# Routing of a fused transformer front: comparison numbers in PSUM, ranks by groups of five tiles, the experts' table on GpSimd

## What is computed

```python
h = tok(x, ...)                                  # patches, class token, positions
h = concatenate([h, txt], axis=1)                # 64 x 69 x 256
h = h + attn(layernorm(h), wq, wk, wv)
h = h + ffn(layernorm(h), router, w13, w2)

# ffn: the two best of eight experts, weighted by a softmax over the two logits
router_logits = x_flat @ moe_router              # 4416 x 8
topk_logits, topk_idx = top_k(router_logits, 2)
topk_weights = softmax(topk_logits)
sort_idx = argsort(topk_idx.reshape(-1))         # 8832 pairs, grouped by expert
w13_out = ragged_dot(x_sort, moe_w13, group_sizes)
hidden = silu(gate) * up
out = ragged_dot(hidden, moe_w2, group_sizes)    # added back to the token's row
```

## Time and profile before

| What | us |
|---|---|
| median of 3 runs | 825.34 |
| lowest and highest run | 822.24, 830.76 |
| the profiled execution, its own time | 829.55 |
| its span, first to last instruction | 827.4 |
| TensorE busy | 724.2 (88%) |
| VectorE busy | 552.7 (67%) |
| ScalarE busy | 418.2 (51%) |
| GpSimd busy | 435.6 (53%) |

### The profile page before, as it was taken

How to read it: one execution, slowest core, us unless ns; L and a number is a source line. 1 busy time by engine, 2 the same in 40 slices (tenths; PEclk the granted TensorE clock), 3 DMA queues, 4 the chain that set the end, 5 groups by cost and what they waited for, 6 DMA issues and landing times. The chain is left out here.

```text
span 827.4 us, 27945 instructions
## 1 busy us (share of the span) xinstructions
PE 724.2 (88%) x9928; PEld 511.9 (62%) x9928; DVE 552.7 (67%) x1163; ACT 418.2 (51%) x951; POOL 435.6 (53%) x602
## 2 busy tenths in 40 slices
PE   6756989998999999989923599999999999999993
PEld 5634667776677776666722266666666666666662
DVE  6975888887888888787668455555555555555552
ACT  1233666677787777787637233333333333333330
POOL 5752554565766565553351255656555555555552
PEclk9985999999999999999655699999999999999997
DMA  8675576555454655454200034333333334343332
GB/s 286 210 240 177 152 244 190 152 163 153 138 163 147 174 159 153 125 169 123 82 25 7 27 54 66 54 64 57 62 59 60 60 59 65 55 66 54 64 55 24
DMA packets 64874, 91.81 MB, mean 111 GB/s; under 512 B 13176, under 2 KB 45704, under 8 KB 64679
## 3 DMA queue, kind: packets, MB, share of 16 engines
q1 hardware_dynamic: 49655, 66.81, 26.7%
q0 software_dynamic: 15088, 23.21, 16.8%
HBM read 58.95 MB, written 24.10 MB: 100 GB/s over the span
## 5 line engine op out<-in xcount | busy, mean ns | idle before, releaser
L1293 POOL DMA_INDIRECT out<-y,token_of x76 | 120.6, 1587 | 133.4 <-DVE own L1361 118.5
L1339 DVE SCALAR_TENSOR_TENSOR hid<-quad,up_scale,silu 128x512 f32<-128x512 f32 x76 | 57.0, 751 | 100.8 <-PE quad L1375 100.8
L1375 PE MATMUL quad<-w_hi,x_hi 128*128 x304 | 116.2, 382 | 1.2 <-DVE x_lo L1346 1.1
L1375 PE MATMUL quad<-w_lo,x_hi 128*128 x304 | 116.2, 382 | 0.0
L1375 PE MATMUL quad<-w_hi,x_lo 128*128 x304 | 116.2, 382 | 0.0
L652 DVE TENSOR_REDUCE nm_src<-quad 69x16 f32<-69x1104 f32 x64 | 83.0, 1297 | 35.4 <-PE quad L1055 35.2
L1307 ACT ACTIVATE hid_hi<-bank 128x512 f16<-128x512 f32 x76 | 45.4, 597 | 103.9 <-PE bank L1394 103.9
L919 ACT ACTIVATE probs<-quad 69x1104 f32<-69x1104 f32 x64 | 69.7, 1089 | 50.5 <-PE quad L1138 50.5
L1280 POOL DMA_INDIRECT wc<-xn_rows,token_of x74 | 73.4, 992 | 33.9 <-issue 21.9
L1375 PE MATMUL bank<-w_hi,hid_hi 128*128 x304 | 82.9, 273 | 1.6 <-ACT hid_hi L1307 1.6
L1375 PE MATMUL bank<-w_lo,hid_hi 128*128 x304 | 82.9, 273 | 0.0
(11 more groups left out here) (230 smaller groups left out, 1866.0 us busy)
## 6 DMA issues: line engine op xcount, KB each, us to landing
w_lo<-in_experts_w SPq DMA_DIRECT2D x24, 512.0 KB, 5.9
w_raw<-in_experts_w SPq DMA_DIRECT2D x48, 256.0 KB, 4.9
xt<-in_patches SPq DMA_DIRECT2D x18, 384.0 KB, 5.7
h<-h_rows SPq DMA_DIRECT2D x34, 128.0 KB, 5.3
hb<-h_rows SPq DMA_DIRECT2D x34, 128.0 KB, 5.7
out<-h SPq DMA_DIRECT2D x34, 128.0 KB, 4.6
xn_rows<-xn SPq DMA_DIRECT2D x34, 128.0 KB, 4.6
vb<-v SPq DMA_DIRECT2D x30, 138.0 KB
```

The lines of the kernel that those rows point to most:

```text
L1293: nc.gpsimd.indirect_dma_start(out, bass.IndirectOffsetOnAxis(token_of[:, n:n + 1], 0), y[q][:, :], None, compute_op=ALU.add).then_inc(add ...
L1339: nc.vector.scalar_tensor_tensor(out=hid[q][:, :], in0=quad[:, 2 * q + 1, :], scalar=up_scale[:, :], in1=silu[q][:, :], op0=ALU.mult, op1= ...
L1375: last = nc.tensor.matmul(dst, x[:, k, :], w[:, bass.ds(col + k * (2 * width if width == HIDDEN else width), width)], start=(k == 0 and m ...
```

## The change

- **Numbers to compare in PSUM.** `lanes` and `places` are copied to bank 0 of `quad` in step 67, and `mark_lanes` and the tile comparisons read them there. The other input stays in SBUF.
- **A step earlier.** `CHOOSE` is step 63, `COUNTED` 64, counting at the end of step 65, `RANK` 66; the constants are written in steps 61 and 62. `lanes` comparisons: two a step in steps 67 to 71, two more behind the loop ahead of the last choice, the last two as before behind the last ranks.
- **Ranks by groups.** `choose_second` sums choices by groups of five tiles (`in_group`) in place of `counts`. `add_places` adds each tile of a group to the later ones of the same group, for all groups at once (four matmuls), and each group's sum to all tiles behind the group (six). The count over all tiles takes seven matmuls in place of two.
- **Who numbers lanes.** GpSimd multiplies groups 9, 10 and 11, one operation of 640 elements each, behind its step loop. ScalarE does 0 to 2 in steps 68 to 70, 3 to 5 behind the loop, then the gates' exponential, then 6, 7, 8, 12 and 13.
- **The table on GpSimd.** `is_expert` comes from two sets of steps, each made by a subtraction, an addition with a lower limit, and an upper limit, on 76 x 8 elements, then a subtraction and a multiplication. `expert_of` is still summed on VectorE, now ahead of its wait for the last placing matmuls.

```diff
-                counts = shift[0][:, 140:148].bitcast(fp16).rearrange("p (a e) -> p a e", a=2)
+                lanes_ps, places_ps = quad[:, 0, 0:P], quad[:, 0, P:P + TILES_MOE]
+                in_group = shift[1][:, 208:236].bitcast(fp16).rearrange("p (b e) -> p b e", e=EXPERTS)
+                both_groups, GROUPS = both.rearrange("p (b g) e -> p b g e", g=GROUP), G // GROUP
-                CHOOSE, COUNTED, RANK = BATCH, BATCH + 1, BATCH + 3
-                LANES = {BATCH + 4 + k: range(3 * k, 3 * k + 3) for k in range(4)}
+                CHOOSE, COUNTED, RANK = BATCH - 1, BATCH, BATCH + 2
+                LANES = {BATCH + 3 + k: range(2 * k, 2 * k + 2) for k in range(5)}
+                LANES_IN_STEPS = 10
+                NUMBER_STEPS = {BATCH + 4 + k: k for k in range(3)}
+                BY_POOL = [9, 10, 11]
...
+                        for n in BY_POOL:
+                            j, b = pair(n)
+                            pool.wait_ge(s["lane_ready"], n + 1)
+                            nc.gpsimd.tensor_tensor(at_lane[n], at_lane[n], field[:, b, None].broadcast_to([P, GROUP, P]), ALU.mult).then_inc(s["pool_scaled"], 1)
                         pool.wait_ge(s["gates"], 2)
...
+                        pool.wait_ge(s["tiles_known"], 1)
+                        nc.gpsimd.tensor_tensor(tile_end, first_tile, tiles_f, ALU.add).then_inc(s["table_parts"], 1)
+                        pool.wait_ge(s["table_parts"], 1)
+                        nc.gpsimd.memset(tile_end[:, EXPERTS - 1:], float(2 * TILES_MOE)).then_inc(s["table_parts"], 1)
+                        pool.wait_ge(s["table_parts"], 2)
+                        for k, (steps_up, edge) in enumerate(((passed, tile_end), (is_expert[:, :, :], first_tile))):
+                            nc.gpsimd.tensor_tensor(steps_up, places[:, :, None].broadcast_to(TE), edge[:, None, :].broadcast_to(TE), ALU.subtract).then_inc(s["table_parts"], 1)
+                            pool.wait_ge(s["table_parts"], 3 + 3 * k)
+                            nc.gpsimd.tensor_scalar(steps_up, steps_up, 1.0, 0.0, ALU.add, ALU.max).then_inc(s["table_parts"], 1)
+                            pool.wait_ge(s["table_parts"], 4 + 3 * k)
+                            nc.gpsimd.tensor_scalar(steps_up, steps_up, 1.0, None, ALU.min).then_inc(s["table_parts"], 1)
+                        pool.wait_ge(s["table_parts"], 8)
+                        nc.gpsimd.tensor_tensor(is_expert[:, :, :], is_expert[:, :, :], passed, ALU.subtract).then_inc(s["table_parts"], 1)
+                        pool.wait_ge(s["table_parts"], 9)
+                        nc.gpsimd.tensor_scalar(is_expert[:, :, :], is_expert[:, :, :], y_scale[:, :], None, ALU.mult).then_inc(s["table_parts"], 1)
                         pool.wait_ge(s["tokens_ready"], 1)
...
-                            nc.vector.tensor_tensor(at_lane[n], lanes[:, None, :].broadcast_to([P, GROUP, P]), lane_f[:, j, b, None].broadcast_to([P, GROUP, P]),
+                            nc.vector.tensor_tensor(at_lane[n], lanes_ps[:, None, :].broadcast_to([P, GROUP, P]), lane_f[:, j, b, None].broadcast_to([P, GROUP, P]),
...
+                            if t == min(LANES):
+                                dve.wait_ge(s["probs_ready"], BATCH)
+                                then(nc.vector.tensor_copy(lanes_ps, lanes))
+                                then(nc.vector.tensor_copy(places_ps, places))
...
                         each(step)
+                        for n in range(LANES_IN_STEPS, LANES_AHEAD):
+                            mark_lanes(n)
                         choose(AHEAD, G)
...
+                        dve.wait_ge(s["table_parts"], 5)
+                        then(nc.vector.tensor_reduce(expert_f, passed, AX.X, ALU.add))
+                        then(nc.vector.tensor_copy(expert_of[:, :], expert_f))
                         dve.wait_ge(s["placed"], PLACED)
...
-                        TE = [P, TILES_MOE, EXPERTS]
-                        then(nc.vector.tensor_tensor(tile_end, first_tile, tiles_f, ALU.add))
-                        then(nc.vector.tensor_tensor(passed, places[:, :, None].broadcast_to(TE), tile_end[:, None, :].broadcast_to(TE), ALU.is_ge))
-                        then(nc.vector.tensor_reduce(expert_f, passed, AX.X, ALU.add))
-                        then(nc.vector.tensor_scalar(expert_f, expert_f, float(EXPERTS - 1), None, ALU.min))
-                        then(nc.vector.tensor_copy(expert_of[:, :], expert_f))
-                        then(nc.vector.tensor_tensor(is_expert[:, :, :], expert_f[:, :, None].broadcast_to(TE),
-                                                        experts_row[:, None, :].broadcast_to(TE), ALU.is_equal))
-                        then(nc.vector.tensor_scalar(is_expert[:, :, :], is_expert[:, :, :], y_scale[:, :], None, ALU.mult))
...
-                            for m in range(lo, min(hi, G - 1)):
-                                behind = G - 1 - m
-                                to = nc.tensor.matmul(b4[:, (m + 1) * EXPERTS:G * EXPERTS].rearrange("p (g e) -> p g e", e=EXPERTS), ones_h,
-                                                      both[:, m, None, :].broadcast_to([P, behind, EXPERTS]), start=False, stop=(m == G - 2), skip_group_check=True)
+                            for m in range(GROUP - 1):
+                                to = nc.tensor.matmul(ranks[:, from_:to_, m + 1:, :], ones_h,
+                                                      both_groups[:, from_:to_, m, None, :].broadcast_to([P, to_ - from_, GROUP - 1 - m, EXPERTS]),
+                                                      start=False, stop=(to_ == GROUPS and m == GROUP - 2), skip_group_check=True)
+                            for b in range(from_, min(to_, GROUPS - 1)):
+                                at = (b + 1) * GROUP
+                                to = nc.tensor.matmul(b4[:, at * EXPERTS:G * EXPERTS].rearrange("p (g e) -> p g e", e=EXPERTS), ones_h,
+                                                      in_group[:, b, None, :].broadcast_to([P, G - at, EXPERTS]), start=False, stop=False, skip_group_check=True)
```

More of the change, by code:

```diff
@@ L159, in front @@
                     denom_ready att_ready h2_ready stats4 mv4_ready eps4 rstd4 off4_ready xn2_ready xn2_turned xn2T_ready logits_mm logits_saved
-                    w_hi_ready w_lo_ready consts chosen gates parts_ready place_mm rank_ready lane_ready lane_scaled tile_found placed tokens_ready weights_stored""".split()
+                    w_hi_ready w_lo_ready consts chosen gates parts_ready place_mm rank_ready lane_ready lane_scaled pool_scaled tiles_known table_parts tile_found placed tokens_ready weights_stored""".split()
                 s = {n: sem("f_" + n) for n in names}
@@ L197, in front @@
                 field, rev = shift[1][:, 160:160 + G], shift[1][:, 200:208]
-                lanes, places, experts_row, spare_id = gain[:, 0:P], gain[:, P:P + TILES_MOE], gain[:, 204:212], gain[:, 212:213]
+                lanes, places, spare_id = gain[:, 0:P], gain[:, P:P + TILES_MOE], gain[:, 204:205]
                 prefix_h, ones_h = (bias[:, at:at + P // 2].bitcast(fp16) for at in (0, P // 2))
@@ L209, in front @@
                 assert len(at_lane) == PLACED
-                CHOOSE, COUNTED, RANK = BATCH, BATCH + 1, BATCH + 3
-                LANES = {BATCH + 4 + k: range(3 * k, 3 * k + 3) for k in range(4)}
-                assert max(LANES) < LAST_STEP and max(LANES[max(LANES)]) == LANES_AHEAD - 1 and back[AHEAD - 1] + 3 < CHOOSE
+                lanes_ps, places_ps = quad[:, 0, 0:P], quad[:, 0, P:P + TILES_MOE]
[6 more added lines that the diff above has]
+                BY_POOL = [9, 10, 11]
+                BY_ACT = [n for n in range(PLACED) if n not in BY_POOL]
+                assert max(LANES) < LAST_STEP and max(LANES[max(LANES)]) == LANES_IN_STEPS - 1 and back[AHEAD - 1] + 3 < CHOOSE
                 def pair(n):
@@ L622, in choose_second @@
                             with nc.allow_low_precision("a token tile counts at most once per row"):
-                                nc.vector.tensor_reduce(counts[:, a, :], both[:, lo:hi, :].rearrange("p g e -> p e g"), AX.X, ALU.add).then_inc(s["chosen"], 1)
+                                nc.vector.tensor_reduce(in_group[:, lo // GROUP:hi // GROUP, :], both_groups[:, lo // GROUP:hi // GROUP, :, :].rearrange("p b g e -> p b e g"),
+                                                        AX.X, ALU.add).then_inc(s["chosen"], 1)
                         def rank(a, lo, hi):
@@ L809, in _ @@
                                                                op0=ALU.is_ge, op1=ALU.mult))
-                        then(nc.vector.tensor_reduce(first_tile, under, AX.X, ALU.add))
+                        nc.vector.tensor_reduce(first_tile, under, AX.X, ALU.add).then_inc(s["tiles_known"], 1)
+                        dve.wait_ge(s["tiles_known"], 1)
                         shape = [P, TOP_K, G, EXPERTS]
@@ L985, in _ @@
                         each(step)
```

(8 more changed lines are left out.)

26 lines of the change are left out of this document (15 added, 11 removed).

## The result

| What | before | changed |
|---|---|---|
| median, us | 826.86 | 821.12 |
| lowest and highest of 20 runs each | 822.24, 831.30 | 812.88, 824.86 |
| span of the profiled execution | 827.4 | 817.3 |

A forecast was written before the change was run, and what follows sets the result against it. From about 400 us to the experts' first matmul at 462.29, the serial chain of last tiles and routing was taken as the bound. Terms 2.7 + 2.2 = 4.9 us, from median 825.34 to 820.4; range 817.5 to 823.5, with rivals 815.5 to 826.0.

The forecast's parts named there:

- step 10: Behind the token list: GpSimd's second gather ends last, first matmul 1.46 us later; 2.2 us more gained.
- signs of being wrong: One-input GpSimd operations over 2 us, table ending behind token list, different stage behind 480 us, another bound before first choice.
- 1 and 2, choice and ranks: Earlier choice and ranks by groups: tile 33 can be normalized at about 414.1, not 415.69; 1.6 us gained.
- 3: VectorE up to the last variance: a comparison from PSUM taken at 0.78 us; variance at 420.5, before 423.1.
- step 4: GpSimd's three small operations need 1.2 us without 6.3 of waiting; VectorE late next; last choice starts 7.4 earlier.
- step 5: GpSimd numbers lanes 9 to 11, 1.6 us each; two choice operations wait 1.3 and 1.4, costing 2.7.
- 7: The 70-wide addition ahead of the tile comparisons waits for a 608-wide GpSimd operation: 1.4 us (0 to 1.5).
- 8: VectorE's reduction and conversion ahead of the token list cost 0.4 us; waiting inside it 0.15, up to 1.3.
- step 9: Table on GpSimd: three two-input operations at 1.5 us, five one-input at 1.0; 11 us, hidden behind token list by 1.8.
- The port is kind: Rival: VectorE's small operations slip in ahead of GpSimd's, so the waits cost nothing; 9.3 us gained, 816.0; chance 0.24.
- GpSimd becomes the bound: Rival: gathers queue behind GpSimd's table, deciding from 2.2 us per operation; at 3.0, 6.4 longer, 831.8; chance 0.12.
- PSUM doesn't free the port: Rival: GpSimd's addition still waits until the last comparison; total 0.6 us gained, 824.7; chance 0.14.

The follow-up runs named there:

- one gather with both back: Changed kernel with lanes back on ScalarE, table back on VectorE, and only the first gather issued ahead of the experts: stretch 55.47 us, ratio to before 0.9898.

## Why the forecast was right, and where it was not

The sign held, and so did the mechanism up to the token list: the chain through the last tile was freed by PSUM, GpSimd's new work gave part of it back. The last term, 2.2 of the forecast's 4.9, did not hold at all (step 10). That the time came out within 0.7 us is luck in part. The forecast was taken from a median of 825.34 over three runs, and over twenty it is 826.86, from which the same 4.9 give 822.0; and errors of over 2 us cancelled. Two of the prediction's own signs of being wrong came: one-input GpSimd operations over 2 us, and table rows that end behind the token list. By steps:

- **1 and 2, choice and ranks.** Tile 33 is normalized 1.8 earlier (15.45 against 17.23; 17.04 in the two later profiles of before), forecast 1.6. The old ranks put back cost 1.9 of it, not 2.8, since the clock is higher behind the longer counting.
- **3.** A comparison with an input in PSUM takes 0.75 (3.00 for four), as from SBUF; 0.78 was taken. The last variance comes 0.6 sooner than forecast.
- **4.** GpSimd needs 1.2 (415.38 to 416.61), and the last choice starts 8.3 earlier, forecast 7.4. SBUF restored in the changed kernel, and PSUM alone in the old one, show that this hangs on where the compared numbers lie and not on the order of the work. Late next is not VectorE alone, as the forecast had it: the last logits come 0.06 behind the last comparison.
- **5.** Both waits are there, one for one as forecast, but a 640-wide f16 operation takes 1.23, not 1.6: they cost 1.6, not 2.7.
- **7.** The wait of the 70-wide addition is 0.6, not 1.4: it met the end of a two-input operation. With step 5 the way from last choice to first tile comparison grew by 2.2 (11.34 to 13.52), forecast 4.2.
- **8.** Ahead of the list 0.4, as forecast. Inside the list 0.15 was taken with a bound of 1.3, and 1.63 was measured (1.18 at L865, 0.45 at L867): mis-sized, beyond its own bound. The list's operations met a two-input operation of 1.46, near the end of a table that ran later than step 9 had it.
- **9.** This size was wrong. One-input operations of 608 elements were taken at 1.0 with 1.5 as the end of the range; they took 2.27, 1.76, 2.25, 1.74 and 1.94. The table takes 15.4 us (432.39 to 447.76) instead of 11 (the step's terms add to 11.5, and its two ends, 438.9 and 450.8, are 11.9 apart), and so ends 1.03 behind the list instead of 1.8 ahead of it. The range had assumed that one input can't cost more than two. The strided row it set aside as a rival's evidence (0.949 for 256, 2.3 at 608) comes near these five, but by chance: it is of a two-input operation, and the table's own of that kind took 1.23 to 1.46.
- **10.** This step named the wrong end. It took the 1.46 between VectorE's last operation and TensorE for a fixed distance behind whatever is last. Behind GpSimd's gather it is 3.6, and in the kernel before both ends met. So taking 3.7 us from VectorE's end gained nothing, where 2.2 were counted: from list to first matmul it is 7.24 against 6.95.

As a sum, in the stretch: 8.3 − 2.2 − 2.0 − 0.3 = 3.8, where the forecast had 7.4 − 4.2 − 0.5 + 2.2 = 4.9. Steps 5 and 7 were 2.0 too dear and step 4 too small by 0.9; steps 8 and 10 were 1.5 and 2.5 too generous.

**The rivals.** *The port is kind*: no; six of VectorE's operations took longer than usual beside GpSimd's. *GpSimd becomes the bound*: in part. The mean of the eight operations is 1.74, below the 2.2 from which it was said to decide, yet its list is what TensorE starts behind. The point itself holds, for two reasons that cancel: the last gather must end 3.65 ahead of 462.29, not 1.46, so with 2.6 from the table's end to the gather's the table must end at 456.1 on the scale of before; and it begins 2.4 sooner than forecast, at 437.9. That is 18.2 for eight operations, 2.2 each with the 0.1 between them. The range "with the rivals" (815.5 to 826.0) left out this rival's own 831.8. *PSUM doesn't free the port*: refuted from both sides.

**What stays open.** The ratio says 6.8 us (4.5 to 9.1), the stretch 3.8, just outside. The stretch behind the first expert matmul doesn't hold the rest (363.3 and 363.7, against 363.1 in two of three profiles of before), and the part ahead of the stretch, where the work is nearly the same, moves by 12 us over the profiles and by 10 us between two of the kernel before. Whether the changed kernel is shorter there on average no run here settles. For the table on VectorE (8.5 by the ratio, 6.8 by the stretch) and for PSUM alone (7.0 and 4.1) the ratio also says more; for one gather with both back they agree (8.4 and 8.4). For comparisons back to SBUF the ratio says 5.8 longer and the stretch 3.7, so what differs is not always on the changed kernel's side.

## What to carry to other kernels

Moving the constant input of a chain of two-input VectorE operations into PSUM costs two small copies and takes GpSimd out of their way; here it alone was worth as much as the whole change. Don't then hand GpSimd wide work beside short serial VectorE work: price its one-input operations from a row of the same form and not below its two-input ones, and count for each serial VectorE operation the length of the one that it may meet. And before you credit a shorter end on one engine, look at which other engine's list meets it at the same time: run the part with one instruction less on that list.

## What the runs showed of the hardware

- On GpSimd a tensor_scalar over 128x608 f32 took 1.74 to 2.27 us, a tensor_tensor of that size 1.23 to 1.46. The Trainium skill (GPSIMD Engine Reference, "When to use GPSIMD") has one-input work at roughly line rate and so as the cheaper kind; by the rows it is the dearer.
- What GpSimd's two-input operations hold on VectorE is held to their end, within 0.1 us: two choice operations, the 70-wide addition, the scalar operation at 444.34, and with comparisons from SBUF the conversion at 458.31 (1.04, up to the end of an operation that ran 457.83 to 459.29). One-input operations held only in their first part. With comparisons from SBUF, the four comparisons that started with one of 1.75 to 2.43 us took 1.03 to 1.07 instead of 0.54 and ended 1.1 to 1.3 us into it, and those behind them took 0.54. In the changed kernel GpSimd ran L549 from 442.44 to 444.18, and VectorE's two-input L864 at 443.25 and 444.07 took 0.24 each. The Trainium skill (SBUF — State Buffer, "Who interferes with whom") gives the lock to any GpSimd operation that reads SBUF. For the other direction the trace agrees (6.58 and 6.01 us for one-element-wide operations beside comparisons from SBUF). For this one it agrees with the two-input operations, and with the one-input ones only for their first 1.1 us or so. The conversion at 446.08 (0.65, up to 0.9 into L553) fits that; the one at 442.01 (0.40, up to the end of L547) does not, and why it waited is open.
- GpSimd's small operation was not let in between two of the comparisons: the 6.58 us from 423.17 to 429.75 reach over eight of them, of 0.75 each.
- A dense run of counting matmuls (4.3 us at 1.2 GHz) was followed by a granted clock of 2.4 GHz in all five profiles that have it, and a short one (1.5 us) in none of nine. Cutting TensorE's counting by 2.8 us so gained 1.9. The clock was never changed by itself, so that the one follows from the other is read from these fourteen profiles and not shown apart.
